# Words of u and y kept in token order, or gathered by step: the layout around a chunked recurrence on one Trainium2 core

## The reference, cut to what matters

```python
x = x + depthwise_shift_conv(layer_norm_over_channels(x))        # called x1
t = tokens(x)                                                    # (2, 65536, 64)
wx = batch_norm(layer_norm(t) @ W.T)                             # u in the kernel, before the batch norm
def step(y, wx_t):                                               # over all 65,536 tokens, in order
    y = sigmoid(wx_t + y @ V.T)
    return y, y
t = t + scan(step, 0, wx)                                        # called x2
# then: linear attention over x2 (x3), and a top-8 routed expert layer over x3
```

## Time and profile before

| | us |
|---|---|
| median of three runs | 1968.5 (1964.88 to 1969.38) |
| the profiled execution | 1974.39 |
| its span, first to last instruction | 1972.3 |
| TensorE / VectorE / ScalarE / GpSimd busy | 1572.6 / 1461.2 / 1269.9 / 1438.2 |
| mean granted TensorE clock | 0.901 |
| stage A | 0 to 759 |
| stage B | 766 to 1079 |

### The profile page before, as it was taken

One profiled execution on the slowest core, in us unless ns is written; L12 is line 12 of the kernel. 1 busy time (PEld: TensorE's weight loads), 2 busy tenths in 40 slices (PEclk: granted clock), 3 DMA queues, 4 the chain that ended last, 5 costly groups with the idle time before them and its releaser, 6 DMA issues. The chain is left out here.

```text
span 1972.3 us, 24751 instructions
## 1 busy us (share of the span) xinstructions
PE 1572.6 (80%) x5690; PEld 652.4 (33%) x5690; DVE 1461.2 (74%) x2373; ACT 1269.9 (64%) x2235; POOL 1438.2 (73%) x1070
## 2 busy tenths in 40 slices
PE   4899999999999972887884969999999999925100
PEld 1333333333333321455551613223222323205100
DVE  1689999999999973788886547999999999941000
ACT  2777777777777651787772468888888888720000
POOL 2999999999999970086776059988998898801570
PEclk8999999999999985999896979999999999955555
DMA  4588788888878656999994067888888887660011
GB/s 152 157 234 254 240 250 249 252 245 249 255 240 253 191 179 187 283 326 364 363 389 196 4 219 247 269 271 270 256 265 273 268 259 241 204 146 14 2 2 1
DMA packets 127392, 429.89 MB, mean 218 GB/s; under 512 B 59632, under 2 KB 64656, under 8 KB 82192
## 3 DMA queue, kind: packets, MB, share of 16 engines
q1 hardware_dynamic: 105568, 423.83, 68.0%
q10 hardware_dynamic: 18736, 4.29, 1.4%
q0 software_dynamic: 2944, 0.18, 0.1%
HBM read 257.93 MB, written 170.01 MB: 217 GB/s over the span
## 5 line engine op out<-in xcount | busy, mean ns | idle before, releaser
L454 ACT ACTIVATE tap_products<-xn,kk 128x512 f32<-128x512 f32 x384 | 275.2, 718 | 165.7 <-POOL x_and_products L485 159.9
L485 POOL TENSOR_TENSOR x_and_products<-tap_products,x_and_products 128x512 f32<-128x512 f32 x256 | 326.7, 1276 | 41.7 <-POOL x_and_products L485 3.5
L385 PE MATMUL pst<-xn,taps 128*128 128x512 f32 x768 | 351.6, 593 | 0.0
L1440 POOL TENSOR_SCALAR exp_q<-exp_q 128x512 f32<-128x512 f32 x128 | 201.4, 1573 | 117.8 <-ACT exp_q L1395 117.8
L910 DVE SCALAR_TENSOR_TENSOR pss<-region,bn,pss 128x256 f32<-128x256 f32 x432 | 196.5, 488 | 69.5 <-PE pss L814 67.7
L849 POOL TENSOR_TENSOR x_block<-x_block,region 128x2048 f32<-128x2048 f32 x28 | 155.2, 5543 | 116.5 <-ACT region L836 82.8
L543 DVE SCALAR_TENSOR_TENSOR pst<-xn,kk,pst 128x512 f32<-128x512 f32 x256 | 191.7, 749 | 61.9 <-PE pst L385 61.7
L385 PEld LDWEIGHTS pst<-xn,taps 128*128 128x128 f32 x768 | 145.4, 190 | 186.2 <-issue 186.0
L485 POOL TENSOR_TENSOR x_and_products<-tap_products,x_ring 128x512 f32<-128x512 f32 x128 | 164.2, 1283 | 20.2 <-ACT tap_products L454 20.2
L1454 POOL TENSOR_TENSOR q_z<-q_map,z_inv 128x512 f32<-128x512 f32 x128 | 163.7, 1279 | 7.1 <-issue 5.2
L425 ACT ACTIVATE sq<-x_ring 128x512 f32<-128x512 f32 x256 | 157.7, 622 | 16.1 <-POOL x_ring L492 10.1
(11 more groups left out here) (243 smaller groups left out, 2996.1 us busy)
## 6 DMA issues: line engine op xcount, KB each, us to landing
rstd_wide<-rstd_scratch SPq DMA_DIRECT2D x128, 512.0 KB, 7.2
x_ring<-in_x SPq DMA_DIRECT2D x32, 1024.0 KB, 5.2
x_scratch<-x_ring SPq DMA_DIRECT2D x32, 1024.0 KB, 4.3
xl_scratch<-wx SPq DMA_DIRECT2D x32, 1024.0 KB, 8.7
region<-xl_scratch SPq DMA_DIRECT2D x32, 1024.0 KB, 11.4
x_ring<-x_scratch SPq DMA_DIRECT2D x32, 1024.0 KB, 8.4
rstd_of_channels<-rstd_scratch SPq DMA_DIRECT2D x64, 512.0 KB, 6.2
x_transposed<-x_squares SPq DMA_DIRECT2D x64, 512.0 KB, 5.0
```

The lines of the kernel that those rows point to most:

```text
L385: m = pe.matmul(wide(pst[g % 2]), taps[:, n * P:(n + 1) * P], tap_rows(g, t), start=(n == 0), stop=(n == len(PE_TAPS) - 1))
L454: act.activation(prod[:, n, :, :], tap_rows(g, t), ACT.Copy, scale=kk[:, t:t + 1]).then_inc(products, 1)
L485: pool.tensor_tensor(xr[:, g % XR, :], prod[:, n, :, :].rearrange("p r w -> p (r w)"), xr[:, g % XR, :] if n else x_tile(g), ALU.add).then ...
L1440: pool.tensor_scalar(e, e, 1.0, None, ALU.min).then_inc(clipped, 1)
```

## The change

u and y are kept in the order of the tokens. `scale_wx` writes straight tiles. `U` becomes `[P, 1 + CHUNKS, CLEN]`, so the words of one step lie 16 words (64 bytes) apart, and the matmuls of L814 in the real steps, all of L910 and L827, the writes of L836 in the real steps and one operand of the check L890 step by 16 words. The loads of a block become one straight row of 8 KB in every partition, the warm load one run of 12 words (48 bytes), and the additions L849 and L922 read y straight. The number of instructions on the compute engines and their order, the semaphores and the waits stay as they are. The sequential repair is changed to match and doesn't run.

```diff
-                    c0 = g % TPB * (TILE // CLEN)
-                    by_chunk = u[:, k % 2, :].rearrange("p (n c) -> p c n", n=CLEN)[:, c0:c0 + TILE // CLEN, :]
-                    dve.tensor_tensor(by_chunk, psw[g % 2][:, :].rearrange("p (c n) -> p c n", n=CLEN),
-                                      rb[1][:, k % 2, cols_of(g % TPB)].rearrange("p (c n) -> p c n", n=CLEN),
+                    dve.tensor_tensor(u[:, k % 2, cols_of(g % TPB)], psw[g % 2][:, :], rb[1][:, k % 2, cols_of(g % TPB)],
                                       ALU.mult).then_inc(u_ready, 1)
...
-        U = [sb(f"region{j}", [P, CLEN, 1 + CHUNKS], F32, regions) for j in range(BUFS)]
+        U = [sb(f"region{j}", [P, 1 + CHUNKS, CLEN], F32, regions) for j in range(BUFS)]
...
             def warm_cols(r, s, j):
-                return U[r % BUFS][:, CLEN - WARM + s, j * GC:(j + 1) * GC]
+                return U[r % BUFS][:, j * GC:(j + 1) * GC, CLEN - WARM + s]
             def step_cols(r, n, j):
-                return U[r % BUFS][:, n, 1 + j * GC:1 + (j + 1) * GC]
+                return U[r % BUFS][:, 1 + j * GC:1 + (j + 1) * GC, n]
...
-                return U[r % BUFS][:, :, c0:c0 + BLOCK // CLEN].rearrange("p n c -> p c n")
+                return U[r % BUFS][:, c0:c0 + BLOCK // CLEN, :].rearrange("p c n -> p (c n)")
...
                 def load_block(r, i):
-                    sp.dma_start(U[r % BUFS][:, :, c0:c0 + BLOCK // CLEN],
-                                 xl_d[r * RBLK + i, :, :].rearrange("p (n c) -> p n c", n=CLEN)).then_inc(...)
+                    sp.dma_start(U[r % BUFS][:, c0:c0 + BLOCK // CLEN, :].rearrange("p c n -> p (c n)"),
+                                 xl_d[r * RBLK + i, :, :]).then_inc(...)
                 def load_warm(r):
-                    sp.dma_start(U[r % BUFS][:, CLEN - WARM:CLEN, 0:1],
-                                 xl_d[r * RBLK - 1, :, :].rearrange("p (n c) -> p n c", n=CLEN)[:, CLEN - WARM:CLEN, BLOCK // CLEN - 1:BLOCK // CLEN],
-                                 allow_slow_non_contiguous=True).then_inc(...)
+                    sp.dma_start(U[r % BUFS][:, 0, CLEN - WARM:CLEN],
+                                 xl_d[r * RBLK - 1, :, BLOCK - WARM:BLOCK]).then_inc(...)
...
-                pool.memset(U[0][:, :, 0:1], 0.0).then_inc(zero_warm, 1)
+                pool.memset(U[0][:, 0, :], 0.0).then_inc(zero_warm, 1)
                 def add_y(r, i, x1_x2):
-                    pool.tensor_tensor(in_chunks(x1_x2), in_chunks(x1_x2), y, ALU.add).then_inc(added, 1)
+                    pool.tensor_tensor(x1_x2, x1_x2, y, ALU.add).then_inc(added, 1)
...
-                    dve.tensor_copy(U[r % BUFS][:, CLEN - 1, 0:1], U[(r - 1) % BUFS][:, CLEN - 1, CHUNKS:CHUNKS + 1])
+                    dve.tensor_copy(U[r % BUFS][:, 0, CLEN - 1:CLEN], U[(r - 1) % BUFS][:, CHUNKS, CLEN - 1:CLEN])
...
-                    dve.tensor_tensor(d, d, U[r % BUFS][:, CLEN - 1, 0:CHUNKS],
+                    dve.tensor_tensor(d, d, U[r % BUFS][:, 0:CHUNKS, CLEN - 1],
...
-                        x1_x2 = in_chunks(last_x1(i))
+                        x1_x2 = last_x1(i)
                         dve.tensor_tensor(x1_x2, x1_x2, y_in_token_order(REGIONS - 1, i), ALU.add).then_inc(last_added, 1)
```

More of the change, by code:

```diff
@@ L705, in last_x1 @@
             def last_x1(j):
-                flat = U[REGIONS % BUFS][:, :, :].rearrange("p n c -> p (n c)")
+                flat = U[REGIONS % BUFS][:, :, :].rearrange("p c n -> p (c n)")
                 return flat[:, j * BLOCK:(j + 1) * BLOCK]
             def warm_cols(r, s, j):
-                return U[r % BUFS][:, CLEN - WARM + s, j * GC:(j + 1) * GC]
+                return U[r % BUFS][:, j * GC:(j + 1) * GC, CLEN - WARM + s]
             def step_cols(r, n, j):
-                return U[r % BUFS][:, n, 1 + j * GC:1 + (j + 1) * GC]
+                return U[r % BUFS][:, 1 + j * GC:1 + (j + 1) * GC, n]
             def ws_at(r, s, j):
@@ L727, in y_in_token_order @@
                 c0 = 1 + i * (BLOCK // CLEN)
-                return U[r % BUFS][:, :, c0:c0 + BLOCK // CLEN].rearrange("p n c -> p c n")
-            def in_chunks(x):
-                return x.rearrange("p (c n) -> p c n", n=CLEN)
+                return U[r % BUFS][:, c0:c0 + BLOCK // CLEN, :].rearrange("p c n -> p (c n)")
             def wait_group(eng, r, j):
@@ L746, in load_block @@
                     c0 = 1 + i * (BLOCK // CLEN)
-                    sp.dma_start(U[r % BUFS][:, :, c0:c0 + BLOCK // CLEN],
-                                 xl_d[r * RBLK + i, :, :].rearrange("p (n c) -> p n c", n=CLEN)).then_inc(region_loaded[r % BUFS][i // GB], 16)
+                    sp.dma_start(U[r % BUFS][:, c0:c0 + BLOCK // CLEN, :].rearrange("p c n -> p (c n)"),
+                                 xl_d[r * RBLK + i, :, :]).then_inc(region_loaded[r % BUFS][i // GB], 16)
                 def load_warm(r):
-                    sp.dma_start(U[r % BUFS][:, CLEN - WARM:CLEN, 0:1],
-                                 xl_d[r * RBLK - 1, :, :].rearrange("p (n c) -> p n c", n=CLEN)[:, CLEN - WARM:CLEN, BLOCK // CLEN - 1:BLOCK // CLEN],
-                                 allow_slow_non_contiguous=True).then_inc(region_loaded[r % BUFS][0], 16)
+                    sp.dma_start(U[r % BUFS][:, 0, CLEN - WARM:CLEN],
+                                 xl_d[r * RBLK - 1, :, BLOCK - WARM:BLOCK]).then_inc(region_loaded[r % BUFS][0], 16)
                 def load_x1(k):
@@ L880, in keep_state @@
                     dve.wait_ge(summed, sum_no[r, WARM - 1, 0])
-                    dve.tensor_copy(U[r % BUFS][:, CLEN - 1, 0:1], U[(r - 1) % BUFS][:, CLEN - 1, CHUNKS:CHUNKS + 1]).then_inc(kept, 1)
+                    dve.tensor_copy(U[r % BUFS][:, 0, CLEN - 1:CLEN], U[(r - 1) % BUFS][:, CHUNKS, CLEN - 1:CLEN]).then_inc(kept, 1)
                 def check_states(r):
@@ L974, in _ @@
                                 pe.wait_ge(seq_y, k * BLOCK + c * CLEN + (n + 1))
-                                pe.matmul(pq[:, :], wT[:, :], xs[:, bass.ds(c + n * (BLOCK // CLEN), 1)], start=True, stop=False)
+                                pe.matmul(pq[:, :], wT[:, :], xs[:, bass.ds(c * CLEN + n, 1)], start=True, stop=False)
                                 pe.matmul(pq[:, :], vT[:, :], ys[:, bass.ds(c * CLEN + n, 1)], start=False,
```

## The result

The changed kernel takes 2056.05 us (median of four runs, 2053.99 to 2057.73), the kernel before 1967.53 in the same series (1964.88 to 1969.38): the ratio is 1.045, 95% interval 1.0432 to 1.0468, 88.5 us slower. I had forecast 2120, 152 us slower. The profiled execution took 2057.73, its span 2055.6, against 1974.39 and 1972.3 before, so between the two traces 83.3 us are to be explained. The profiled execution of the kernel before is slower than all four runs of this series, 7 us above their median; a difference of a few us against that trace alone decides nothing.

A forecast was written before the change was run, and what follows sets the result against it. Stage B was taken as bound by its recurrence, three full engines and a chain without slack. The terms -1.6 - 3.1 + 156 + 4.7 - 4 = +152 us, against 1968.5, gave 2120 us, range 2030 to 2225.

The forecast's parts named there:

- the step costs on all three engines: Recurrence in stage B: VectorE, ScalarE and TensorE all pay, 1.8 to 2.5 ns a word; the main forecast, chance 0.47.
- C: Stage B: the 64-byte step is free and transfers hold the stage, so straight rows give 1939 to 1960 us; chance 0.06.
- the end: End of stage B: the last additions by GpSimd and VectorE, now straight, save 0.9 and 3.1, together 4 us.
- I take 2.2, since 8 words is the nearest step to it, on every port: Price of a strided word on VectorE, ScalarE and TensorE: 2.2 ns, against 1.04 straight on VectorE and 0.79 on ScalarE.
- the lower end: L910's strided read of u priced at 1.79 ns a word: +0.19 us an instruction, in place of +0.30.
- rival A: L814: the matmul doesn't feel the step, VectorE and ScalarE do; 2095 us, at the cheapest 2044; chance 0.25.
- rival B: L814: the matmul fetches its words for each of four passes, 2.25 us each; 2354 us; chance 0.08.
- the longer of the busiest engine and the latency: Full slot in stage B: latency 3.15 us, just over TensorE's 3.12, so the slot grows by 1.36 us.
- three engines for full: Two-region slots before the change: VectorE 4 x 0.447, ScalarE 4 x 0.455, TensorE about 4 x 0.43 us, no slack.
- The check's price: L890 in VectorE's queue before L910: eight subtractions of 512 words at 1.16 ns more a word, +4.7 us.
- the rest of the DMA time saved is hidden: Loads of stage B: beyond 3.1 us saved in the first slots, straight transfers shorten nothing, as the recurrence sets the pace.
- D: TensorE in stage B: longer slots lower the matmul clock to 1.2 GHz, another 0.8 us a slot; 2200 us; chance 0.09.

The follow-up runs named there:

- rem_dve: Changed kernel with VectorE reading 256 neighbouring words of a constant buffer in place of strided u: 2046.47 us, ratio 1.0399 to the kernel before.
- rem_act: Changed kernel with ScalarE writing the real steps as neighbouring words into other buffers: 2014.22 us, of which 35 us lie behind stage B and prove nothing.
- add_dve: Kernel before with only L910 reading its 256 words 16 apart, from a constant buffer: 1989.55 us, ratio 1.0114.
- add_pe: Kernel before with only the matmuls after a real step reading words 16 apart, from a constant buffer: 2062.1 us, ratio 1.0478.
- the short one: Separate kernel without the computation, timing 256-word instructions with words 1 to 64 apart on three engines; VectorE 483 ns straight, 671 at 16 words.
- rem_pe: Changed kernel with TensorE reading 256 neighbouring words of a constant buffer in place of strided y: 2030.35 us, ratio 1.0316 to the kernel before.
- add_act: Kernel before with only L836 writing its real steps 16 words apart, into a separate buffer: 1979.09 us, ratio 1.0057.

## Why the prediction was right in direction and too large

**Right: that the step costs on all three engines, and that nothing on the other side pays for it.** L903, L829 and L807 all rose and the straight `warm_state` writes did not; no run shows C's free step. L568 came to 690 ns, stage A shortened by 1.9 us (forecast 1.6), the end by 4.4 (forecast 4), L915 to 2.28 us undisturbed, as forecast. The first loads ran at 416 GB/s, and the second group started 5.2 us earlier by them (forecast 3.1).

**Wrong, the step that failed: "I take 2.2, since 8 words is the nearest step to it, on every port", in place of 1.79.** The measured prices over straight words are 0.65 ns on VectorE in the kernel ((655 - 489) / 256; 0.75 by the lower end, 1.16 taken), and 0.90 on ScalarE ((703 - 474) / 256; 1.41 taken). The 2.18 ns drawn from L1675 and L1676 divided two short instructions of different shape, 64x64 and 64x8. The long instructions of the same engines as the ones that change, L568 beside L520, said 0.77. The matmul was taken at 1.13 us and is 0.87: 0.44 more than a straight one, not 0.70. That rules out rival A (no cost) and rival B (2.25 us), and it fits a single fetch for each of the two records: 2 x 256 x 1.69 ns = 0.87 (estimate, with VectorE's price of a strided word in the kernel, 1.04 + 0.65). The prediction had this form and the wrong price; no run shows the fetches themselves.

**Half right: the longer of the busiest engine and the latency.** I took three engines for full, which VectorE and ScalarE were not, added 0.70, 0.30 and 0.36 to one slot of latency and found 3.15, just over the busiest engine, 3.12. With the measured 0.44, 0.17 and 0.23 that latency is 2.63, and TensorE's own work 2.60: again near each other, and the slot is the longer of the two, as I had taken it. But I let the latency set it, and rem_dve and rem_act, whose latency falls while the slot stays at 2.59, show that where two regions run TensorE does. The slot rose by 0.81 in place of 1.36. 98 x 0.81 + 14 x 0.94 = 93 in place of 152, and this is nearly the whole miss, 59 of 64 us. The check's price by itself was smaller than I had it: 0.87 in place of 0.55 us, +0.32 each, where the forecast was 0.6. What it waits for GpSimd decides more, and I had left that to the range: the seven checks before the last take 23.7 us together, and took 22.2. Against the early regions of before, whose checks took 1.8, one is 1.6 dearer; against the late ones it is mostly cheaper.

**Wrong: "the rest of the DMA time saved is hidden".** From the shares and waits I read that the recurrence set the pace and the transfers kept up. They did in the first half of the stage; in the second they cost 4 us a region, by way of GpSimd and the check, and straight loads by themselves are worth 14 us by the medians; in the traces 5 of them fall before the first copy (834.35 us against 839.58), the rest in the late regions. The row said so: 1.01 busy, and a wait of GpSimd of up to 7.5 us; I took them for harmless since GpSimd was "ahead" on average. So a region costs 13.2 us more than one of the first three of before (43.5 against 30.3: 14 slots at 0.81 to 0.94, and 1.6 in the check), but only 9.5 more than one of the last three (34.0), and of 6 x 13.2 = 79 us the traces show 68. The same comparison goes with add_dve, which cost 23 and not 45: its regions are 34.0 us apart throughout, 3.7 above the early ones of before and no more than the late. The last region gives the rest: 14 slots at 0.94 would be 13 us, and the traces show 8.5 from the last copy to the last link, for in before its first slots, too, ran at the lower clock and took 2.31 us. That add_pe is 6 us slower than the full change I can only put together, not show: it has the slots, but not the faster loads and additions, and its check takes 5.6 to 5.7 us; its last region is quicker.

**D, the clock:** granted 0.50 in the last region and 0.89 in 860 to 1040 us (0.92 before). It fell as D has it, but cost little there. At the upper level the last region's slot would be 2.57 (the sum above), so that 2.73 makes some 2 us in 14 slots (estimate). The 0.8 us a slot that D names is seen only behind the checks, where four links take 3.4 us in place of 2.60; that lasts for two to three slots a region (897.87 to 906.25 us), and the kernel before has such links too.

## What to carry to other kernels

Price a strided access from the longest instruction of the same engine that has one, never from the difference of two short ones. Then ask of each slot whether it is one engine's work or one link's latency: in the first case only the fullest engine's extra counts (here that of the matmul's read: by itself it moved the stage's mark by 91 us, and the whole change moved it by 87), in the second all add up. And when a share of a resource reads 1.0 in the stage, take its bound as the next one close by, even if nobody on the critical path waits for it: both a slowdown and a gain will be cut short by it.

## What the runs showed of the hardware

- A float32 matmul of 256 columns whose moving words are 16 words apart takes 0.87 us in the kernel and 0.93 in the short one, in place of 0.43 and 0.50; 2 words apart it costs next to nothing (L320 and L323 have eight records in 1.99 and 2.08 us, L338 in 3.70). At the lower clock a straight one takes as long: behind the check all links stand 0.86 us apart (902.05, 902.90), and the last region's slot at clock 0.50 is 2.73 us with the step and without it (after and rem_pe). From the upper level of the clock to 0.50 the last region's slot grows by 0.52 to 0.53 us with straight matmuls (before, add_act, add_dve) and by 0.11 with strided ones (add_pe, rem_dve, rem_act): the strided read hardly depends on TensorE's clock.
- The price by the step is no price by distance: free at 2 words, a part at 3, full from 4 words on, with a bump at 24 on all three engines and a smaller one at 32 on VectorE (754 ns) and at 64 on ScalarE (757). The Trainium skill, "SBUF — State Buffer", in the section "Door 1: The DMA port swizzle", wants two or more hits in a line of 16 bytes for full rate, which fits 2, 3 and 4 words; the same note's "4 fp32" as the step that is still free does not (672 ns at 4 words, 483 at 1).
- GpSimd's addition of 2048 words, one input in rows of 16 single words 513 apart, is only 22% dearer than straight (5.54 against 4.56 us).
- VectorE's check subtraction, two inputs in SBUF, never ended before the GpSimd addition that was running when it began, but 0.55 us behind it (0.87 with a strided input). So its record grew from 0.68 us (add_act at 876.50, where no addition ran) to 5.7 (add_pe), according to how much of the addition was left. Where two engines shut each other out, a late transfer on one becomes a stall on the other.
